# Seven cast weight groups instead of six, a third stream slot, a 4 KB descriptor ring and two re-gated loads in a slot-attention layer on eight cores

## What is computed

```
x = x + layernorm(cumulative_mean(layernorm(x)))
y = layernorm(x)
h = gelu(concat(y, mean(S)) @ w1 + b1)                  # 512 wide
a = top-8 softmax of (h @ w2 + b2) / (|tau| + 0.1)      # 64 slots per row
si = (a^T @ y) / (sum of a + 1e-8)                      # 64 x 1024
gi, gh = si @ Wih^T + bih, S @ Whh^T + bhh              # GRU gates r, z, n
S' = GRU(S, gi, gh)
q, k, v = S' @ wq, S' @ wk, S' @ wv;  S' = layernorm(S' + softmax(q k^T / 16) v)
x = x + layernorm((a @ (S' @ wvp + bvp)) @ wo + bo)
```

## Time and profile before

| | us |
|---|---|
| median of 3 runs | 321.55 (320.13 to 321.61) |
| the profiled execution, own time | 320.65 |
| its span on the slowest core (core 7) | 319.1 |
| spans of the eight cores | 312.9 to 319.1 |

### The profile page before, as it was taken

The page is one execution under the profiler, slowest core; times in us unless marked ns, Lnnn a source line. Parts: engine busy times, 40 slices in busy tenths (PEclk is TensorE's granted clock), DMA queues, the critical chain, the costliest instruction groups (busy, mean ns, idle before and its releaser), DMA issues.

```text
span 319.1 us, 5787 instructions; the slowest of 8 cores (312.9 to 319.1 us)
## 1 busy us (share of the span) xinstructions
PE 225.5 (71%) x1806; PEld 130.5 (41%) x1806; DVE 198.1 (62%) x358; ACT 178.1 (56%) x332; POOL 165.2 (52%) x236
## 2 busy tenths in 40 slices
PE   0033763995998989969799778963758892888720
PEld 0000333672775767747676477620233330111100
DVE  0378935798787897898955654420222403999970
ACT  0133631786688896997989764400202015999830
POOL 3877681686487878999797641000000001656530
PEclk9999989797999999999999799995577997555555
DMA  6999999999999996999999981599999300999998
GB/s 158 262 233 171 171 211 234 258 258 236 249 229 268 236 198 86 137 128 155 112 115 95 110 126 35 75 248 204 180 315 264 75 0 0 361 341 350 351 366 339
DMA packets 24784, 63.33 MB, mean 198 GB/s; under 512 B 1926, under 2 KB 2438, under 8 KB 24754
## 3 DMA queue, kind: packets, MB, share of 16 engines
q0 software_dynamic: 11376, 22.22, 50.1%
q1 hardware_dynamic: 12576, 40.18, 38.0%
q10 hardware_dynamic: 802, 0.57, 0.7%
HBM read 68.40 MB, written 23.07 MB: 287 GB/s over the span
## 4 chain that ended last, share of the span: by engine, by line
PE 34%; DMA 24%; DVE 17%; ACT 14%; issue 7%; POOL 1%; DVEq 0%; ACTq 0%; SPq 0%; POOLq 0%
PE R L369 9%; DVE sb_x L867 9%; DMA x3b_s<-w1b 9%; DMA wsl<-wbf 8%; DMA sb_x<-x 6%; PE R L534 4%; ACT junk L338 3%; ACT junk L323 2%; PE R L353 2%; PE R L309 2%; ACT x1b L859 2%; PE R L314 2%; PE R L473 2%; PE R L453 2%; ACT L436 2%
## 5 line engine op out<-in xcount | busy, mean ns | idle before, releaser
L369 PE MATMUL R<-xT,w1a_s 128*128 128x256 bf16 x512 | 65.7, 277 | 1.1 <-DVE Lb L415 1.1
L369 PEld LDWEIGHTS R<-xT,w1a_s 128*128 128x128 bf16 x512 | 50.9, 100 | 11.4 <-issue 2.3
L346 POOL TENSOR_SCALAR x3b_s<-sb_x,nm,vr 128x1024 bf16<-128x1024 f32 x32 | 38.4, 1201 | 12.8 <-PE R L453 4.3
L334 DVE SCALAR_TENSOR_TENSOR sb_x<-R,sqs,sb_x 128x1024 f32<-128x1024 f32 x32 | 40.7, 1272 | 5.9 <-POOL sqs L331 5.9
L338 ACT ACTIVATE junk<-sb_x,nm 128x1024 bf16<-128x1024 f32 x32 | 36.5, 1140 | 10.4 <-DVE sb_x L334 10.4
L867 DVE SCALAR_TENSOR_TENSOR sb_x<-R,sqs,sb_x 128x1024 f32<-128x1024 f32 x32 | 38.9, 1283 | 3.3 <-POOL sqs L865 3.3
L300 POOL TENSOR_SCALAR x1b<-sb_x,nm,r 128x1024 bf16<-128x1024 f32 x32 | 39.1, 1226 | 1.6 <-POOL r L294 1.3
L323 ACT ACTIVATE junk<-R 128x1024 bf16<-128x1024 f32 x32 | 32.5, 1015 | 10.5 <-PE R L319 10.0
L851 PE MATMUL R<-svd,aT 64*128 64x512 bf16 x64 | 29.5, 582 | 11.5 <-DVE sb_x L867 8.9
L859 ACT ACTIVATE x1b<-R 128x1024 bf16<-128x1024 f32 x32 | 32.7, 1023 | 5.3 <-PE R L851 2.1
L309 PE MATMUL R<-x1b,cmat 128*128 128x512 bf16 x60 | 19.9, 417 | 20.1 <-DVE sb_x L334 18.4
(11 more groups left out here) (156 smaller groups left out, 342.6 us busy)
## 6 DMA issues: line engine op xcount, KB each, us to landing
out<-sb_x SPq DMA_DIRECT2D x32, 512.0 KB, 8.1
sb_x<-x SPq DMA_DIRECT2D x15, 1024.0 KB, 24.9
wbf<-wmid POOLq DMA_DIRECT2D x6, 1024.0 KB, 18.8
sb_x<-whh POOLq DMA_DIRECT2D x4, 1024.0 KB, 52.7
wsl<-wmid POOLq DMA_DIRECT2D x4, 1024.0 KB, 14.5
msl<-wbf SPq DMA_DIRECT2D x4, 1024.0 KB, 21.1
wsl<-whh POOLq DMA_DIRECT2D x2, 1024.0 KB, 87.7
msl<-wmid POOLq DMA_DIRECT2D x2, 1024.0 KB, 16.8
```

What stands on the lines that cost most here:

```text
L334: kx2[j] = DV.put(lambda v: v.scalar_tensor_tensor(xs(j), RR[j % 2][:], s2[:, j:j + 1], xs(j), op0=OP.mult, op1=OP.add), ks2[j], kx1[j])
L346: kx3[j] = PO.put(lambda g: g.tensor_scalar(x3s(j), xs(j), nm[:, j:j + 1], r3[:, j:j + 1], op0=OP.add, op1=OP.mult), t, kx2[j], ksi.get(j ...
L369: PE.quiet(lambda e, jc=jc, dc=dc, ob=ob, q=q: e.matmul(ob, w1a[:, dc * H + jc * P:dc * H + (jc + 1) * P], xT[:, dc * 2 * P:(dc + 1) * 2 * ...
```

## The change

Five edits. The descriptor scratch of POOL's DMAs is 4096 bytes per partition instead of the default 16384. NW is 3 instead of 2, so the stream has seven slots: three in `wsl`, one in `x1b`, three in `msl`. Group 7 is cast by way of DRAM too, and the casts move to iterations 7, 8, 11, 12, 13, 14, 15. x tiles 8 and 9 wait for w1a and tiles 10 on for w1b. The whh groups of gates z and n are issued in iterations 0 and 2 instead of at the start.

```diff
-NW = 2
+NW = 3
...
-    nc = bass.Bass("TRN2", target_bir_lowering=False)
+    nc = bass.Bass("TRN2", target_bir_lowering=False, dynamic_dma_scratch_size=4096)
...
-        load_x(8, 2, kw1b)
-        for a in range(10, 24, 2):
+        load_x(8, 2, kw1a)
+        load_x(10, 2, kw1b)
+        for a in range(12, 24, 2):
             load_x(a, 2)
-        kwh = {g: [group("whh", whh_at[g][:, u * GC * D:(u + 1) * GC * D], whh_d[g, u]) for u in range(2)]
-               for g in range(3)}
+        kwh = {}
+
+        def load_whh(g):
+            kwh[g] = [group("whh", whh_at[g][:, u * GC * D:(u + 1) * GC * D], whh_d[g, u]) for u in range(2)]
+
+        load_whh(0)
...
-        CAST_AT = {7: (4,), 9: (5,), 11: (6,), 12: (8,), 13: (10,), 14: (11,)}
+        WHH_AT = {0: 1, 2: 2}
+        CAST_AT = {7: (4,), 8: (5,), 11: (6,), 12: (7,), 13: (8,), 14: (10,), 15: (11,)}
...
+            if i in WHH_AT:
+                load_whh(WHH_AT[i])
+            if i == 6:
+                tw[2] = group("wm", slot(2), wmid_d[2])
...
             if i == 10:
-                for g in range(NW):
+                for g in range(2):
                     tw[g] = group("wm", slot(g), wmid_d[g], tt["slots"])
```

## The result

The changed kernel takes **324.65 us** (median of 20 runs, 321.93 to 329.53), the kernel before 321.18 in the same 20 rounds: ratio 1.0101, 95% interval 1.0077 to 1.0124. It is slower by 3.2 us, where 319.5, 2 us faster, was forecast.

The account below looks back on a forecast made before the run. It took tail DMA loads ahead of q and k as the bound: 320.65 - 2.0 = 318.65 us, plus 0.9 for the median, 319.5 forecast. Its forecast case spanned 317.5 to 319.9 (0.34); 8 in 10, 312 to 327.

Parts of the forecast that it names:

- the comparison of 235.2 with 237.24: Start of q and k (L750): forecast at 235.2 us against 237.24 in the profiled execution, so 2.0 us less.
- the backlog of q0: End of stage A: one direct group and one cast more, 16.7 us less 2.0 filled; last cast lands at 201.4 us.
- The tail: q1's loads before q and k, starting near 200 us: g3 lands at 212.4, `spk` at 229.0, q and k 6.2 later.
- PE waits for g3 beyond 214 us: Sign of being wrong, in PE's tail: g3 was forecast to land at 212.4 us.
- The x stall: Stage A's start: earlier x8 ends DVE's wait, 3.6 us earlier on core 7, counted at nothing in the sum.
- The room runs over: Rival, DMA gaps cannot be filled: `spk` at 231 to 232.7 us, end moves -0.2 to +1.7, 320.3 to 323; chance 0.28.
- The gate of g12: Rival, tail: g12's packets stand between g6 and `spk`, q and k at 241, 324.5 to 326 us; chance 0.17.
- The ring: Rival, POOL's smaller descriptor scratch: if only three large transfers fit, issues stop, +6.3, 328 us; chance 0.09.
- The waits fall together: Rival, tail: q1 gets ahead of q0, `spk` by 218 us, q and k at 224, 309.7 us; chance 0.12 with what lies between.

Follow-up runs that it names:

- e10: The kernel before with only the 4 KB ring and the four later whh DMAs issued in iterations 0 and 2; ratio 1.0011 to before.
- e7: The changed kernel with group 7 loaded directly (six casts) and x8 gated on w1b as before; 309.0 us, ratio 0.9599 to before.
- e6: The kernel before with only a seventh cast (group 7) added, still two slots; ratio 1.0009 to before.
- e4: The changed kernel with x tiles 8 on waiting for w1b as before; 322.72 us, ratio 1.0057 to before.
- e1: The changed kernel with group 7 loaded directly, six casts instead of seven; 312.99 us, ratio 0.9727 to before.
- e3: The kernel before with only the 4096-byte descriptor scratch, all six whh DMAs still issued at the start; one run, 330.23 us.
- e12: The changed kernel with groups 7 and 11 direct (five casts) and x8 gated on w1b; ratio 0.9617 to before.
- e2: The kernel before with only the x gates changed: tiles 8 and 9 wait for w1a, tiles 10 on for w1b; ratio 1.0023 to before.
- e5: The changed kernel with the loads of spk, cps and bqk ahead of g6 in SP's queue; ratio 1.0134 to before.

## Why the prediction was wrong

With e10 neutral, four kernels with x8 gated on w1b form a table of two by two (the two on the right have the small ring and the late whh issues as well, g2 in iteration 6 and g5's cast in iteration 8; in all but the kernel before, the casts of g8, g10 and g11 stand one iteration later):

| | two slots | three slots |
|---|---|---|
| six casts | 1 (before) | 0.9599 (e7) |
| seven casts | 1.0009 (e6) | 1.0057 (e4) |

The slot alone is worth 4.0%. The cast alone is worth nothing. Together they lose, because both draw on the same still stretch of DMA: from 194 to 204 us its share is 0.71 in e7's mean and 1.01 in e4's, and e4's seventh cast runs on into the tail. The stretch was shorter than core 7 of before made it look (0.05 there); the mean of the eight cores is 0.42, some 6 us of room and not 10. Core 0 of the same execution:

```profile
194.00:204.00 10.00, 9.73 (x128) 6.28 (x129) 4.55 (x13) 4.04 (x5) 0.80 (x1) 1.00 0.65 116
```

*The mechanism in one count.* q1's loads in front of q and k are g4, g5, g6 and `spk`, 3 x 33 + 9 = 108 packets per engine, issued from 196 to 197 us in e4 and e7 alike. What differs is what q0 puts between them. Queues of core 7 from 200 to 210 us, e4 and then e7:

```profile
q0 software_dynamic: 374, 0.74, 52.1%
q1 hardware_dynamic: 696, 1.40, 48.3%
```

```profile
q1 hardware_dynamic: 1634, 2.71, 89.2%
q0 software_dynamic: 29, 0.06, 3.6%
```

In e7 the last cast lands at 191.2 in the mean and g3 at 197.4, so q1 has the engines to itself; `spk` lands at 212.0, 15.3 us after the issue of g4. In e4 the last cast lands at 205.5, g3 (215.6) and the direct g9 stand behind it, and `spk` lands at 229.0, 32.7 us after. Between g4's issue and `spk` q0 passes 3.5 packets per engine in e7 and 78 in e4, means of the eight cores. At 0.22 us a packet the difference is 16.4 us by my estimate; `spk` came 17.0 us later, for 14.3 us more of backlog.

*The step that failed first: the comparison of 235.2 with 237.24.* The forecast took q and k of the slowest core of one execution as what the change starts from, and worked out the new time largely from rates, which know nothing of that core's delays. The table shows the two like for like: 232.5 before in the mean of the cores, 234.5 after (234.9 in e4), the output 2.4 us later (2.0 in e4). The forecast 235.2 is within 0.7 us of both, and "2.0 us less" should have read 2.7 us more, which gives 324.3 in place of 319.5. Cores 6, 0 and 3 above would have shown that core 7 of the execution before was not the place to subtract from. The rest of the way, from e4's 1.8 us over before to the changed kernel's 3.2, is the early x8, if it is more than noise.

*The step that was mis-sized: the backlog of q0.* The forecast added 16.7 - 2.0 = 14.7 us to the landing of the last cast, 186.7 to 201.4. Measured, like for like: core 7 went to 211.1, 24.4 us more; the means went from 183.1 to 207.3, 24.2 more (205.5 in e4). The runs split the 24.2 in four. The ring and the late whh issues (before to e10) make 2.1, priced at nothing. The slot's direct load, with the casts moved (e10 to e7), makes 6.0, priced at 7.1. The seventh cast (e7 to e4) makes 14.3, priced at 9.55; alone in the kernel before (before to e6) it makes 13.4. The early x8 (e4 to the changed kernel) makes 1.8, priced at nothing. Some 0.5 us a cast is in the row that was chosen: core 7 passed 1327 packets in the earlier trace rows, two other cores of the same execution, 6 and 3, in the same 24 us:

```profile
q0 software_dynamic: 1203, 2.39, 98.1%
...
q0 software_dynamic: 1215, 2.41, 100.0%
```

The mean of the eight is 1254, 10.1 us a cast. Whether the 2 us of gaps were filled can't be told from these numbers.

*The tail.* Forecast for `spk` 229.0, measured 228.4 (229.0 in e4). That this came out although the backlog was some 9 us too small is in part luck. The forecast let q1 start at 200 us and gave it 29 us to `spk`, past 37 + 33 + 9 = 79 packets of q0 per engine (of cast and g3, of g9 and of g12). In e4's mean the first load was issued at 196.3 and the way took 32.7 us, past 78 packets, with more of the casts among them: the start came 3.7 us sooner and the way was 3.7 us longer. From `spk` to q and k: forecast 6.2, measured 5.5 on core 7 (236.18 - 230.70) and 5.9 in e4's means. On core 7 the wait for g6 is gone, the wait for `spk` stands in its place, and v has no wait, as forecast; cores 1 and 2 wait 1.53 and 5.53 us for g8. g3 is not as forecast: due at 212.4, it landed at 220.0 on core 7. "PE waits for g3 beyond 214 us" was one of the signs of being wrong that the prediction named, and the row of 220.14 us above shows it.

*The x stall.* x8 landed 12.2 us after an issue near 30 us, the sum over w1b started as before, and DVE found x8 there, as forecast for 46.5 us. PE and DVE of core 7:

```profile
40.54 1.91 PE L493 MATMUL R<-x3b_s,smT 128*64 128x512 bf16 x8
```

```profile
45.65 0.69 DVE L288 BATCH_NORM_STATS2 bn<-sb_x 128x6 f32<-128x512 f32 x1
```

The stall of the earlier trace rows is gone, and counting its 3.6 us at nothing was right for the tail. What failed is that the price of the early x8 ended at w1b. It is carried on: the last cast lands 1.8 us later (e4 to the changed kernel), 3.7 us with six casts (e7 to e1), and the kernel loses 0.4% (intervals overlapping) and 1.3%.

*The rivals.* The room runs over: `spk` at 231 to 232.7 did not come in the mean, and the end moved further than its +1.7. The gate of g12: its time, 324.5 to 326, holds the measured 324.65 and its longer backlog came, but not its mechanism: q and k stand at 234.9 in e4's mean and not at 241. g12 was issued more than 5 us ahead of `spk`'s landing on two cores of e4 (0 and 1: 220.3 and 220.0 us, `spk` at 227.2 and 230.4), and `spk` was no later there than on the six others (227.2 to 231.0). The ring: the forecast set three large transfers that fit against seven, both without a row for it. e3 shows seven, with a stop of 13.21 us ahead of the eighth on core 0. The changed kernel never met the stop; POOL's issues on core 7:

```profile
11.88 1.50 POOL L235 DMA_DIRECT2D sb_x<-whh  x2
22.15 1.55 POOL L235 DMA_DIRECT2D sb_x<-whh  x2
40.53 1.56 POOL L235 DMA_DIRECT2D wsl<-whh  x2
```

*The waits fall together* named the other side of the threshold, `spk` by 218 us and then 309.7. e7 lands it at 212.0 and takes 309.0. The rival was right on what decides, and this change does not reach it. That e7 comes so near its number is in part chance: the rival counted seven casts, e7 has six.

Open: why one more cast moves the last one by 13.4 us with two slots and 14.3 with three, and not by 10.1. That eight cores cast at once may be part of it, but no run here takes one core alone.

## What to carry to other kernels

Before two edits are stacked that both fill the same idle stretch of a queue, add up what the stretch holds; one may be worth 4% and both together less than nothing, and leaving one entry out is the experiment that shows it. Leave out more than one in turn: which entry it is can matter as much as how many. Where two queues share the engines, ask first whether one is empty when the other's urgent loads begin: 11 us more of backlog below that point (e12 to e7) moved `spk` by nothing, 14 us more beyond it (e7 to e4) by 17 us. And a path is to be subtracted from the mean of the cores, not from the slowest core of one execution, when the new value comes from rates.

## What was not expected of the hardware

**An early x load slows what follows.** e7 and e1 differ only in x8's gate. Windows of 46 to 90 us, cores 2, 3 and 7 of e7 and then of e1:

```profile
46.00:90.00 44.00, 36.38 (x328) 25.58 (x329) 36.24 (x74) 27.88 (x55) 29.01 (x33) 0.92 1.05 249
46.00:90.00 44.00, 36.50 (x330) 25.06 (x328) 35.85 (x72) 28.86 (x56) 27.52 (x32) 0.91 1.04 248
...
46.00:90.00 44.00, 38.28 (x341) 26.73 (x339) 36.85 (x77) 30.32 (x59) 28.79 (x34) 0.91 1.05 250
```

```profile
46.00:90.00 44.00, 39.91 (x352) 27.79 (x351) 37.16 (x76) 30.24 (x59) 30.97 (x37) 0.89 1.03 229
46.00:90.00 44.00, 39.77 (x350) 27.72 (x351) 37.00 (x77) 30.01 (x58) 29.65 (x35) 0.89 1.05 243
...
46.00:90.00 44.00, 38.97 (x354) 27.81 (x355) 38.08 (x78) 30.38 (x59) 30.24 (x36) 0.92 1.04 233
```

The engines are full in both, but move 247 GB/s in the mean of the eight cores with the late gate and 238 with the early one. Before and e2 (247 and 238), e4 and e5 (245 and 238) say the same. The changed kernel against e4 shows less of it (241 and 245), and e10, with the late gate, has 242, one execution each. Why they move less there is open.

**Cores drift apart by their DMA.** With the same instructions on all eight cores, the last cast lands between 193.5 and 220.2 us in the profiled execution of the changed kernel, its longest of 20. In ordinary executions the spread is smaller: 8.7 us in e4 (200.4 to 209.1) and in e7 (186.9 to 195.6), 13.6 in e5. That a backlog widens it is not shown.
